# A decoder layer on one core: two transposes and three copies change their order, and an epsilon moves into a column of the squares

## The reference

```python
x = x + gla(ln(x))          # recurrent (gated linear) attention, 16 heads
x = x + cross(ln(x), ctx)   # cross attention, 16 heads, 112 keys and 16 extra ones
x = x + ffn(ln(x))          # 4 experts, each takes its best 512 of the 2048 tokens
```

```python
mu = o.mean(-1, keepdims=True)
var = ((o - mu) ** 2).mean(-1, keepdims=True)
o = (o - mu) * jax.lax.rsqrt(var + EPS)          # EPS = 1e-5
return jax.nn.silu(gproj) * o @ Wo.T
```

## Time and profile before

| | us |
|---|---|
| three runs | 958.82, 959.66, 960.10 |
| median | 959.66 |
| the profiled execution, its time | 958.86 |
| the profiled execution, its span | 957.1 |
| attention stage in it, about | 0 to 560 |
| PE busy, share of the span | 888.1, 93% |
| DVE busy | 676.7, 71% |
| POOL busy | 473.7, 49% |
| ACT busy | 447.0, 47% |
| mean granted clock of TensorE | 0.988 |

### The profile page before, as it was taken

One profiled execution on the slowest core, in us unless ns is written; L12 is line 12 of the kernel. 1 busy time (PEld: TensorE's weight loads), 2 busy tenths in 40 slices (PEclk: granted clock), 3 DMA queues, 4 the chain that ended last, 5 costly groups with the idle time before them and its releaser, 6 DMA issues.

```text
span 957.1 us, 19632 instructions
## 1 busy us (share of the span) xinstructions
PE 888.1 (93%) x7569; PEld 508.7 (53%) x7569; DVE 676.7 (71%) x1313; ACT 447.0 (47%) x748; POOL 473.7 (49%) x532
## 2 busy tenths in 40 slices
PE   1788999999999999999999888999999999999995
PEld 0455666666666666666665544444444444444442
DVE  6887888888888888888886749665554454445962
ACT  3645665666556665666656633222332233223210
POOL 1657877787877878778772310110720010005833
PEclk9988999999999999999999999999999999999998
DMA  8614000000000000000022035223462343246683
GB/s 271 195 56 140 5 20 18 21 3 18 18 16 18 3 18 16 18 14 8 18 68 91 13 122 209 89 88 108 113 176 89 119 155 121 88 129 202 184 260 103
DMA packets 42415, 81.90 MB, mean 86 GB/s; under 512 B 11778, under 2 KB 12098, under 8 KB 42370
## 3 DMA queue, kind: packets, MB, share of 16 engines
q1 hardware_dynamic: 37378, 66.58, 21.3%
q0 software_dynamic: 4992, 14.70, 5.5%
HBM read 67.62 MB, written 13.65 MB: 85 GB/s over the span
## 4 chain that ended last, share of the span: by engine, by line
PE 53%; POOL 23%; DVE 11%; issue 7%; ACT 4%; DMA 1%; POOLq 1%; SPq 0%; DVEq 0%; ACTq 0%
PE ps L1192 15%; PE ps L1194 15%; PE ps L1193 15%; POOL hrs L672 6%; POOL pr L732 4%; PE ps L1198 2%; POOL hrs L670 2%; POOL rstd L657 2%; POOL dk L688 1%; PE ps L1403 1%; POOL kraw L714 1%; POOL pr L734 1%; POOL od L706 1%; POOL gate L700 1%; PE ps L1364 1%
## 5 line engine op out<-in xcount | busy, mean ns | idle before, releaser
L1165 ACT ACTIVATE big<-ps 128x512 f32<-128x512 f32 x64 | 38.2, 597 | 226.7 <-PE ps L1194 226.7
L2226 DVE TENSOR_SCALAR big<-big 128x512 f16<-128x512 f32 x64 | 27.9, 437 | 109.0 <-ACT big L1165 105.7
L1192 PE MATMUL ps<-big,w1h 128*128 128x512 f16 x256 | 97.1, 379 | 0.8 <-DVE big L1703 0.8
L1192 PE MATMUL ps<-w2h,big 128*128 128x512 f16 x256 | 97.0, 379 | 0.3 <-DVE big L1703 0.2
L1194 PE MATMUL ps<-big,w1l 128*128 128x512 f16 x256 | 97.0, 379 | 0.0
L1193 PE MATMUL ps<-w2l,big 128*128 128x512 f16 x256 | 97.0, 379 | 0.0
L1193 PE MATMUL ps<-big,w1h 128*128 128x512 f16 x256 | 97.0, 379 | 0.0
L1194 PE MATMUL ps<-w2h,big 128*128 128x512 f16 x256 | 97.0, 379 | 0.0
L828 POOL DMA_INDIRECT y_fetched<-y_scratch,idx_get x32 | 39.8, 1245 | 96.9 <-DMA y_scratch<-big 87.4
L811 POOL DMA_INDIRECT big<-x_scratch,token_of x16 | 17.2, 1078 | 136.7 <-PE ps L1198 77.6
L672 POOL TENSOR_TENSOR hrs<-hvar,neg_half 128x16 f32<-128x16 f32 x28 | 81.3, 2917 | 1.4 <-DVE hvar L1774 1.4
(11 more groups left out here) (346 smaller groups left out, 2436.7 us busy)
## 6 DMA issues: line engine op xcount, KB each, us to landing
wst<-in_w SPq DMA_DIRECT2D x28, 1024.0 KB, 5.3
x_scratch<-xn SPq DMA_DIRECT2D x16, 256.0 KB, 2.1
y_fetched<-in_w SPq DMA_DIRECT2D x4, 1024.0 KB, 14.4
out<-x_all SPq DMA_DIRECT2D x4, 1024.0 KB, 6.8
pr<-in_w_attn SPq DMA_DIRECT2D x3, 1024.0 KB, 8.4
x_all<-in_w_attn SPq DMA_DIRECT2D x3, 1024.0 KB, 11.4
x_all<-in_x SPq DMA_DIRECT2D x1, 3072.0 KB, 11.6
y_scratch<-big SPq DMA_DIRECT2D x12, 256.0 KB, 4.4
```

Of the source, the lines that this page charges most:

```text
L1165: act.activation(hg[f % 2], psum[f % 2][:, 512:1024], ACT.Gelu, scale=UN).then_inc(hg_r, 1)
L1192: nc.tensor.matmul(o, lh, rh, start=first, stop=False)
```

## The change

1. PE: the fourth part of the probabilities (`b2_turn` 3) is transposed ahead of the keys (`b1_kT`) instead of behind them; `b2_pv` goes ahead of `a1_kg1`; the queries (`b1_qT`) go ahead of the recurrent outputs (`a2_o_turn`).
2. ACT: `kg1_out` goes from ahead of `k_out` to behind `c_hi`; `q_out` goes ahead of `o_square`.
3. `o_square` writes no longer into `od` but into a view `osq` with 33 columns per head, whose first column holds 32 times epsilon. It shares its storage with `ksq` (a tile `hsq` with 34 columns per head: `osq` is columns 0 to 32, `ksq` columns 1 to 33). `head_var` 0 sums over all 33, so POOL's addition into `hve` is left out and `head_deviation` 0 is a single instruction. In the drain the bias of ACT's Ln and the constant of DVE's refinement become 0.
4. At the start one memset is added (`osq`'s column) and three are left out (`eps_head`). No DMA is added, removed or moved.

```diff
-        hve = sb("hve", [P, HEADS])
-        eps_head = sb("eps_head", [P, 3, HEADS])
...
-        ksq = sb("ksq", [P, HEADS, DV + 1])
+        hsq = sb("hsq", [P, HEADS, DV + 2])
+        osq, ksq = hsq[:, :, 0:DV + 1], hsq[:, :, 1:DV + 2]
...
+            pool.memset(osq[:, :, 0:1], DV * EPS_HEAD[0])
...
-                pool.memset(eps_head[:, n, :], DV * EPS_HEAD[n])
...
-                if n == 0:
-                    pool.tensor_tensor(hve[:, :], hvar[0][:, :], eps_head[:, 0, :], ALU.add).then_inc(hdev[0], 1)
-                    after(pool, hdev[0], b, nth=1, per=2)
-                    pool.tensor_tensor(hrs[0][:, :], hve[:, :], neg_half[:, :], ALU.pow).then_inc(hdev[0], 1)
-                else:
-                    pool.tensor_tensor(hrs[n][:, :], hvar[n][:, :], neg_half[:, :], ALU.pow).then_inc(hdev[n], 2)
+                pool.tensor_tensor(hrs[n][:, :], hvar[n][:, :], neg_half[:, :], ALU.pow).then_inc(hdev[n], 2)
...
-                square(od[:, :], b1, o_ps, s[0], hq[0])
+                square(osq[:, :, 1:DV + 1], heads(b1), o_ps, s[0], hq[0])
...
-                on(s[0], kg1_out)
                 on(s[2], k_out)
                 on(s[3], c_hi)
+                on(s[0], kg1_out)
+                on(s[2], q_out)
                 on(s[1], o_square)
-                on(s[2], q_out)
                 on(s[0], log_sigmoid)
...
                 on(s[3], b2_turn, 2)
+                on(s[3], b2_turn, 3)
                 on(s[2], b1_kT)
-                on(s[3], b2_turn, 3)
+                on(s[3], b2_pv)
                 on(s[0], a1_kg1)
-                on(s[3], b2_pv)
+                on(s[2], b1_qT)
                 on(s[1], a2_o_turn)
-                on(s[2], b1_qT)
                 on(s[0], a1_kg2)
...
-                on(s[1], head_var, 0, od)
+                on(s[1], head_var, 0, osq)
```

More of the change, by code:

```diff
@@ L1061, in head_deviation @@
                 after(act, hv[n], s[0])
-                act.activation(hln[n][:, :], hvar[n][:, :], ACT.Ln, bias=eps_head[:, 0, 0:1] if n == 0 else 0.0).then_inc(hdev[n], 1)
+                act.activation(hln[n][:, :], hvar[n][:, :], ACT.Ln, bias=0.0).then_inc(hdev[n], 1)
                 after(act, hdev[n], s[0], nth=1, per=2)
@@ L1773, in head_var @@
                 after(dve, hq[n], s[0])
-                dve.tensor_reduce(hvar[n][:, :], sq[:, :, :] if n else heads(sq[:, :]), AX.X, ALU.add).then_inc(hv[n], 1)
+                dve.tensor_reduce(hvar[n][:, :], sq[:, :, :], AX.X, ALU.add).then_inc(hv[n], 1)
             def head_norm(s, n, dst, src, done, scale=1.0):
@@ L1974, in refined @@
                 after(dve, hdev[n], s[0], nth=2, per=2)
-                chained(dve.scalar_tensor_tensor(newton[n][:, :], hvar[n][:, :], 0.0 if n else DV * EPS_HEAD[0], hrs[n][:, :], ALU.add, ALU.mult))
+                chained(dve.scalar_tensor_tensor(newton[n][:, :], hvar[n][:, :], 0.0, hrs[n][:, :], ALU.add, ALU.mult))
                 chained(dve.scalar_tensor_tensor(newton[n][:, :], newton[n][:, :], -0.5, hrs[n][:, :], ALU.mult, ALU.mult))
@@ L2001, in drain @@
                 b2_low(p)
-                head_var(r, 0, od)
+                head_var(r, 0, osq)
                 refined(r, 0)
```

## The result

The changed kernel takes **969.69 us** (median of 4 runs, 968.89 to 972.97) against 959.88 for the kernel before in the same comparison: ratio 1.0114, 95% interval 1.0088 to 1.0139. It is slower, as forecast, but by 9.8 us and not by 6.2; the time lies 0.09 us above the upper end of the range. The profiled execution is the one of 970.22 us, span 968.5, which is 11.4 more than the span of before.

A forecast was written before the change was run, and what follows sets the result against it. Two paths, over PE and over POOL, were taken to arrive together at the gated outputs' transpose. Terms 2.9 + 1.7 + 1.6 = 6.2 us on 958.86 gave 965.1, or 965.9 against the median; range 961.2 to 969.6.

The forecast's parts named there:

- The steady body: Repeating loop body: the square behind the queries' copy delays POOL's power; 0.22 us slower per body, 2.9 us over 13.
- the hand-over from DVE's sums to the power: Steady body: wait between the end of DVE's sums and POOL's power, taken as 0.08 us, putting the power at 205.58.
- t = 2: Body with late queries: squares queue behind their copy; gated outputs' transpose 1.7 us later, plus 1.6 us for the clock.
- The slack: Steady body, transpose of the gated outputs: the POOL path has 0.13 us to spare, the PE path none.
- the 0.40 us on the scores: Steady body: queries ahead of the recurrent outputs bring copy and scores 0.40 us earlier, lost again as PE's wait.
- It doesn't reach the queries: Steady body: the probabilities ahead of the keys win at most 0.51 us, up to c_hi, and nothing for the queries.
- At nothing: Moves costed at zero: kg1 and its copy behind b2_pv and c_hi, the start-up memsets, the drain constants.
- the clock: Body t = 2: PE's longer wait drops its clock to half speed for a stretch; 1.6 us lost.
- The rival in which the clock holds: Body t = 2: no stretch at half clock, so 1.6 us less, 964.3 us; chance 22%.
- The port: Rival, steady body and t = 2: DVE's instructions hold POOL's power through shared SBUF interfaces; 1.9 us more, 967.8; 13%.
- The rival's price per body: Steady body: the power held by DVE's small ctl, costing 0.07 to 0.08 us per body, 1.0 us in 13; rival's chance 13%.
- The addition left out. It saved the 0.37 us: Every body: dropping POOL's addition saves 0.37 us from hve to the power, which still starts 0.35 us later.

The follow-up runs named there:

- e6: Kernel before with only the fourth part of the probabilities ahead of the keys, and kg1 and its copy behind b2_pv and c_hi: 961.61 us, ratio 0.9957.
- e7: Changed kernel with probabilities and kg1 back in their old places; queries first, copy ahead of the square, and epsilon column stay: 976.11 us, ratio 1.0120.
- e2: Changed kernel with PE and ACT steps back in the old order, so only the epsilon column and the left-out addition remain: 960.87 us, ratio 1.0013.
- e3: Changed kernel with recurrent outputs turned and squared ahead of the queries again, on PE and ACT: 956.67 us, ratio 0.9967.
- e9: Kernel before with one line moved: the fourth part of the probabilities turned ahead of the keys, kg1 left in place: 959.68 us, ratio 0.9971.
- e8: Changed kernel with the old order of queries and recurrent outputs, on PE and ACT, in the body t = 2 alone: 969.00 us, ratio 1.0049.
- e12: Second run of the changed kernel with the old order of queries and recurrent outputs in the body t = 2 alone: 967.74 us, ratio 1.0048.
- e1: Kernel before with the new order of PE and ACT steps alone; POOL's epsilon addition and the square in od stay: 971.89 us, ratio 1.0139.
- e11: The changed kernel measured once more, unaltered, against the kernel before: 970.22 us, ratio 1.0077.

## Why the prediction was right in kind and short in size

**The steady body: right mechanism, 0.30 instead of 0.22.** The steps fell as worked out: copy at 7.26 (forecast 7.27), square at 7.93 (7.94), no hold by the port, a wait of PE of 0.57 (0.6). The mis-sized term is the hand-over from DVE's sums to the power. I took 0.08, from the sums to `hve`. In the traces of before and after the power itself starts 0.14 behind its sums (77.03 to 77.17 in t = 2 before), so 9.40 and not 9.34. The slack was as read: POOL's gated product ended 0.44 later behind the pair (14.99 instead of 14.55), of which 0.03 came between the power and that end, and the transpose started 0.31 later. Over twelve bodies 3.65, with 0.21 in the drain 3.9, against 2.9; within the bounds of 1.3 to 5.2.

**Where the 0.40 us on the scores came from: wrong.** "It doesn't reach the queries" was the step on the probabilities, and the gain on the scores was put down to the queries' order. e6 and e7 show it the other way round. With the probabilities ahead, `b2_pv` and `kg1` end early enough for the recurrent outputs to start being turned before DVE has the queries (6.04 and 6.50 in e6), so both paths come forward by 0.42 with the old order of queries and squares. Queries first buys 0.26 on the copy by itself (e7, 7.41) and nothing beside the other part (e6), and it moves the square back by 0.90 us without the probabilities' part (8.08 in e7, 7.18 in e2) and by 1.18 with it (7.93 after, 6.75 in e3). For the sum it made no difference: in both accounts the copy follows DVE's queries, and there the forecast of 7.27 was sound. For what to keep of the change it makes all the difference. "At nothing" for `kg1` was wrong likewise (e9).

**t = 2: right, to 0.1 us.** 1.69 for the transpose (forecast 1.7), 1.63 for the clock (1.6), and e8 and e12 tie both to that swap. That the clock would fall at all was taken over from an earlier stretch and not derived, so there is luck in it. The rival in which the clock holds is out, in all five profiled executions with that order in t = 2 (31.33 to 31.46 us, and 33.66 with the held power).

**The port: not where I looked.** In the steady body nothing is held. In t = 2 the power started at 87.60, 0.07 ahead of `wl`, and took 2.92. I had written that it would start about 0.1 ahead as well (84.41 against 84.54) and yet be held. It did hit in e1, where the addition pushed the power into `wl` (t = 2 2.2 us longer than in the changed kernel). The rival's price per body, 0.07 to 0.08, never fell due.

**t = 1: the failed step, a term that was put at nothing.** "The addition left out. It saved the 0.37 us" was costed as a saving for every body, and t = 1 was not opened at all, although already had a power held by `wl` in t = 2. Leaving it out there lets POOL's product run into DVE's `xn`, on which PE waits. In six executions with an addition (e9 left out) the stretch takes 33.07 to 33.56 us, in seven without it 34.31 to 35.39: means 33.30 and 34.67, so 1.4 us, with no overlap. The two longest had the longest stretches at half clock. With 3.9 for the bodies and 3.3 for t = 2 this makes 8.6 us; the medians differ by 9.8, with an interval from 8.4 (0.0088 of 959.88). The rest, 1.2 us, no run places, and it needn't belong to the change: in e11's comparison the same two kernels differ by 7.4 us, less than the 8.6. That the time came to lie just above the range, and not just inside it, is therefore partly chance. That a term of 1.4 us was missing isn't: the traces of thirteen executions show it.

## What to carry to other kernels

Where two paths end at one instruction, a step moved ahead must be charged to the path it is moved past, and its gain checked against the other moves of the same change: the useful half here was the one costed at nothing, and e6, which keeps the kernel before and moves only probabilities and `kg1`, is the version to keep. Every body that isn't like the steady one has to be looked at by itself, since a removed delay can change there which instructions run side by side. And a gain of a few us in a kernel whose clock can fall for 10 us is read from distances in the trace, with the times beside them.

## What the runs showed of the hardware that I had not expected

In these traces POOL's small power is held by DVE's 128x2048 two-input instruction only when it starts inside it. Over the 14 traced executions, in t = 1: seven powers started 0.07 to 0.21 us ahead of `wl` and took 2.92 to 3.06 us; seven started 0.12 to 0.24 us behind its start and took 4.85 to 4.96, until `wl` had ended and nearly a whole power more. In t = 2 nine started 0.07 to 0.08 ahead and took 2.92, and five 0.24 inside and took 4.83 or 4.84. There was no exception. The Trainium skill, GPSIMD Engine Reference, section Specifications, has the two engines share their SBUF interfaces; these rows agree, and show which of them gives way. `wl` itself took 2.30 or 2.31 us in all of them, so a power that starts first doesn't hold DVE.

Beside a larger POOL product each engine loses once: `xn` takes 3.42 us instead of 2.37 in all seven executions without the addition, the gate product 1.74 instead of 1.26. Taken one by one, the instructions of the changed kernel's t = 1 show the same order of starting. The product starts at 45.43, inside the first `xn` (44.83 to 46.04), and ends 1.13 behind it. The second `xn` starts at 45.97, inside the product, takes 2.28 us instead of 1.21, and ends 1.08 behind the product. So a delay of a third of a microsecond on POOL could be worth 1.4 us.
